# A Mamba-2 mixer between two LoRA layers: programs written out, and x transposed directly behind the mixing

## What is computed

```python
proj = hidden_states @ in_proj_w.T                     # 512 -> 18560
gate, xBC, dt = jnp.split(proj, [INTER, INTER + CONV_DIM], axis=-1)
conv = causal depthwise convolution of xBC, 4 taps, + conv_b
xBC = jax.nn.silu(conv)
x, Bm, Cm = jnp.split(xBC, [INTER, INTER + NG * SS], axis=-1)
dt = jnp.clip(jax.nn.softplus(dt + dt_bias), DT_MIN, DT_MAX)
cs = jnp.cumsum(dt * A)                                # by head
scores = (C . B) * exp(cs_l - cs_s), lower triangle    # by head
y = scores @ (x * dt) + x * D
yg = y * jax.nn.silu(gate)
out = (yg * rsqrt(mean(yg ** 2) in each of 8 groups)) * norm_w
x = x + out @ out_proj_w.T
```

## Time and profile before

| | us |
|---|---|
| runs before, median of 3 | 1664.43 |
| lowest and highest | 1662.55, 1666.53 |
| profiled execution | 1663.83 |
| its span | 1662.0 |
| its mean granted TensorE clock | 0.985 of full speed |

### The profile page before, as it was taken

One profiled execution on the slowest core, in us unless ns is written; L12 is line 12 of the kernel. 1 busy time (PEld: TensorE's weight loads), 2 busy tenths in 40 slices (PEclk: granted clock), 3 DMA queues, 4 the chain that ended last, 5 costly groups with the idle time before them and its releaser, 6 DMA issues. The chain is left out here.

```text
span 1662.0 us, 27199 instructions
## 1 busy us (share of the span) xinstructions
PE 1579.7 (95%) x8296; PEld 1228.1 (74%) x8296; DVE 1314.3 (79%) x1689; ACT 1025.0 (62%) x2122; POOL 1071.0 (64%) x790
## 2 busy tenths in 40 slices
PE   6979999999999999999999999999999999999879
PEld 4657777777777777777777777777777777777657
DVE  6689877887788777887788777887788777887565
ACT  4467766656666666666666665666666565666431
POOL 2028884777658784777648784787657784788520
PEclk9899999999999999999999999999999999999979
DMA  3033322223222222222222221222222221222011
GB/s 115 1 108 118 106 77 71 89 91 90 71 77 90 88 80 70 90 90 71 78 89 89 67 89 58 97 89 84 77 73 90 89 90 58 89 90 83 20 39 51
DMA packets 73709, 132.16 MB, mean 80 GB/s; under 512 B 10944, under 2 KB 10944, under 8 KB 73280
## 3 DMA queue, kind: packets, MB, share of 16 engines
q1 hardware_dynamic: 73536, 130.09, 23.8%
HBM read 127.44 MB, written 2.62 MB: 78 GB/s over the span
## 5 line engine op out<-in xcount | busy, mean ns | idle before, releaser
L159 PE MATMUL bank<-h_hi,mx_w_hi 128*128 128x512 f32 x1152 | 481.1, 418 | 23.7 <-issue 21.8
L161 PE MATMUL bank<-h_hi,mx_w_lo 128*128 128x512 f32 x1152 | 455.5, 395 | 0.0
L160 PE MATMUL bank<-h_lo,mx_w_hi 128*128 128x512 f32 x1152 | 452.2, 393 | 0.0
L839 POOL TENSOR_TENSOR mx_w_lo<-mx_w_raw,mx_w_hi 128x512 fp32r<-128x512 f32 x144 | 365.1, 2536 | 112.2 <-ACT mx_w_hi L834 112.1
L1113 ACT ACTIVATE mx_mix<-mx_csb,mx_gncs 128x256 f32<-128x256 f32 x512 | 219.1, 499 | 277.6 <-PE bank L1480 254.2
L892 DVE SCALAR_TENSOR_TENSOR mx_acc<-bank,mx_cw,mx_acc 128x510 f32<-128x510 f32 (+2 forms) x480 | 356.5, 743 | 30.5 <-ACT mx_acc L877 19.2
L1267 DVE TENSOR_TENSOR mx_mix<-mx_mix,mx_cbt 128x1536 f32<-128x1536 f32 x128 | 356.2, 2783 | 0.0
L159 PEld LDWEIGHTS bank<-h_hi,mx_w_hi 128*128 128x128 f32 x1152 | 217.8, 189 | 83.2 <-issue 46.3
L1285 DVE SCALAR_TENSOR_TENSOR mx_y<-mx_acc,mx_dh,bank 128x512 f32<-128x512 f32 x128 | 95.7, 747 | 207.6 <-PE bank L1480 185.1
L1038 POOL TENSOR_TENSOR mx_y<-mx_y,mx_sg 128x512 f32<-128x512 f32 x128 | 213.5, 1668 | 69.4 <-DVE mx_y L1285 60.1
L161 PEld LDWEIGHTS bank<-h_hi,mx_w_lo 128*128 128x128 f32 x1152 | 217.4, 189 | 50.0
(11 more groups left out here) (163 smaller groups left out, 2183.9 us busy)
## 6 DMA issues: line engine op xcount, KB each, us to landing
mx_csb<-cs_rows SPq DMA_DIRECT2D x128, 512.0 KB, 4.0
mx_w_raw<-in_w_in SPq DMA_DIRECT2D x144, 256.0 KB, 4.1
mx_wo_raw<-in_w_out SPq DMA_DIRECT2D x64, 256.0 KB, 4.2
res<-in_x SPq DMA_DIRECT2D x8, 256.0 KB, 3.6
f_base_raw<-in_base_wt SPq DMA_DIRECT2D x2, 1024.0 KB, 5.9
out<-res SPq DMA_DIRECT2D x8, 256.0 KB, 2.0
f_a_raw<-in_lora_a SPq DMA_DIRECT2D x2, 256.0 KB, 3.0
f_lb_raw<-in_lora_b SPq DMA_DIRECT2D x2, 256.0 KB, 6.7
```

Source lines behind the costliest of these rows:

```text
L159: nc.tensor.matmul(out, w_hi, x_hi, start=first, stop=False)
L160: nc.tensor.matmul(out, w_hi, x_lo, start=False, stop=False)
L161: return nc.tensor.matmul(out, w_lo, x_hi, start=False, stop=last)
L839: self.nc.gpsimd.tensor_tensor(self.w_lo[:, w % 3, :, :], self.w_raw[:, w % 3, :, :], self.w_hi[:, w % 3, :, :].bitcast(F32), ALU.subtract ...
```

## The change

It does five things.

1. `loop_halves` is replaced by `groups_in_turn`: the programs of TensorE, ScalarE and VectorE are written out for all 8 groups, with no loop.
2. TensorE: `transpose_x` comes first in a step, directly behind the mixing of the step before, and the projection of unit st + 5 behind it. Unit 5 is projected in the tail, between `project` 4 and the second `b_dot_c`, and no longer in step 0.
3. VectorE: the `silu_conv` of a step's start moves to the end of the step before, behind `silu_gate`: step st now makes the SiLU of unit st + 5 (in step 15: of unit 0 of the next group). That of unit 4 closes the tail.
4. VectorE: `inverse` moves from the end of the tail to step 0 of the next group, behind its `silu_conv`.
5. ScalarE's tail: `evacuate` 3 goes ahead of `tanh_conv` 2, and `evacuate` 4 ahead of `round_w` 3.

```diff
-        def loop_halves(eng, steps, tail):
-
-            half = XT + 1
-            steps(0, range(half), True)
-            with eng.Fori(0, NG - 1) as g:
-                steps(g, range(half, STEPS), True)
-                tail(g, True)
-                steps(g + 1, range(half), True)
-            steps(NG - 1, range(half, STEPS), False)
-            tail(NG - 1, False)
+        def groups_in_turn(steps, tail):
+
+            for g in range(NG):
+                steps(g, g + 1 < NG)
+                tail(g, g + 1 < NG)
...
@@ scalar, tail
                     evacuate(g + 1, 2)
+                    evacuate(g + 1, 3)
                     tanh_conv(g + 1, 2)
-                    evacuate(g + 1, 3)
                     tanh_conv(g + 1, 3)
+                    evacuate(g + 1, 4)
                     ip.round_w(act, g + 1, 3)
-                    evacuate(g + 1, 4)
                     tanh_conv(g + 1, 4)
...
@@ vector, before the steps, in a step, in the tail
+            silu_conv(0, 4)
...
                     if st >= 1:
                         skip_y(g, st - 1)
-                    silu_conv(g, st + 4)
                     make_mix(g, st)
                     scale_x(g, st)
...
                     silu_gate(g, st)
+                    if here or more:
+                        silu_conv(gn, un)
                     if st % 2 == 1:
                         split_wo(g, st // 2)
+                    if st == 0 and not first(g):
+                        inverse(g - 1)
...
                 if more:
-                    silu_conv(g + 1, 0)
                     head_constants(g + 1)
...
                     keep_bc(g + 1, 1)
-                    inverse(g)
+                    silu_conv(g + 1, 4)
...
@@ tensor, before the steps, in a step, in the tail
             ip.project(pe, 0, 4)
+            ip.project(pe, 0, 5)
             b_dot_c(0, 1)
...
-                    if st + 1 < STEPS:
+                    transpose_x(g, st)
+                    if 0 < st < STEPS - 1:
                         ip.project(pe, g, st + 5)
-                    elif more:
+                    elif st == STEPS - 1 and more:
                         ip.project(pe, g + 1, 0)
-                    transpose_x(g, st)
                     project_gate(g, st)
...
                     ip.project(pe, g + 1, 4)
+                    ip.project(pe, g + 1, 5)
                     b_dot_c(g + 1, 1)
```

More of the change, by code:

```diff
@@ L1170, in _, with steps @@
             tanh_conv(0, 4)
-            def steps(g, these, more):
-                for st in these:
+            def steps(g, more):
+                for st in range(STEPS):
                     here = st + 1 < STEPS
@@ L1232, in tail @@
                     next_ln.root(act, 1)
-            loop_halves(act, steps, tail)
+            groups_in_turn(steps, tail)
         @block.vector
@@ L1419, in tail @@
                     add_group(NG, 7)
-            loop_halves(dve, steps, tail)
+            groups_in_turn(steps, tail)
         @block.tensor
@@ L1493, in project_out @@
                     pe.wait_ge(s["gsum"], 1 + TT * g + p - 1)
-                elif isinstance(g, int) and g == NG:
+                elif g == NG:
                     pe.wait_ge(s["gcopy"], 1 + TT * g - 1 + p)
@@ L1550, in tail @@
                     project_out(NG, 7)
-            loop_halves(pe, steps, tail)
+            groups_in_turn(steps, tail)
 def program(nc, x, w_in, w_dt, conv_w, conv_b, dt_bias, d_skip, norm_w, w_out, base_wt, router_wt, lora_a, lora_b,
```

## The result

| | before | after |
|---|---|---|
| median of 4 runs, us | 1665.48 (1662.55 to 1670.57) | 1625.80 (1624.96 to 1627.01) |
| profiled execution, us | 1663.83 | 1627.01 |
| its span, us | 1662.0 | 1625.2 |

The ratio is 0.9759, with a 95% interval of 0.9734 to 0.9785. The change gains 36.8 us between the two spans and 39.7 us between the medians. 27.7 us were forecast, counted from the profiled execution, and the time lies 2.2 us under the range.

The account below looks back on a forecast made before the run. The prediction took TensorE, busy 1579.7 of 1662.0 us, to bound the kernel. From the profiled execution, 1663.83 - 24.6 - 5.3 - 1.45 + 3.65 = 1636.1 us, with a range of 1628 to 1643.

Parts of the forecast that it names:

- Part 1, jumps: Loop jumps between steps 8 and 9 of groups 1 to 6: writing loops out removes stalls and slow stretches, -24.6 us.
- Part 2, joints: Seven joints of two groups: project 5 fills a gap and transposes come earlier, 0.75 us each, -5.3 us.
- the chain of unit 5: Joint, step 1: ScalarE's table loads, root and evacuation delay unit 5's SiLU to 661.2, limiting the gain to 0.75 us.
- Part 3: Step 15 of group 7: the transposes' wait for the SiLU of unit 19 goes, -1.45 us.
- Part 4, chain in group 0: Steps 0 to 7 of group 0: without output projection the SiLU chain makes steps 8.15 us, +3.65 us.
- Part 4, switches: Transposes behind the mixing in 120 steps: five uncovered weight loads before and after, 0 us, bounds ±0.06 us a step.
- Cheaper in front: Rival: the chain doesn't bind in group 0 and joints gain 1.1 us, 1630 us; chance 0.12.
- The dear switch: Rival: going from mixing straight to transposes costs extra 120 times, 1648 us at 0.10, 1672 at 0.30; chance 0.07.

Follow-up runs that it names:

- e1: The kernel before with its three loops written out and no instruction moved; 1639.58 us, ratio 0.9853.
- e2: The changed kernel with the loops of the kernel before kept, all moves made; 1659.09 us (median of ten), ratio 0.9973.
- e6: The changed kernel with the reciprocal (`inverse`) back in VectorE's tail, ahead of the SiLU of unit 4; 1638.51 us, ratio 0.9851.
- e11: The changed kernel with the transposes between the gate projection and the output projection; 1609.61 us (one run).
- e3: The changed kernel with the transposes of x behind the projection again in every step, VectorE's SiLU left in its new place; 1626.51 us, ratio 0.9782.
- e4: The changed kernel with the transposes behind the projection in steps 0 to 7 of group 0 alone; 1620.33 us, ratio 0.9749.
- e8: The changed kernel with the SiLU of unit 4 ahead of the copy of B·C in VectorE's tail; 1626.13 us, ratio 0.9787.
- e9: The changed kernel with ScalarE's root behind the tanh of unit 5 and VectorE's reciprocal moved to step 1; 1625.24 us, ratio 0.9774.

## Why the prediction was wrong, point by point

**Part 1, jumps: right**, size included (e1). The clause that three slow stretches go with them is right as well. What it missed is that a jump's price depends on what surrounds it: 31.1 us in e2.

**Part 2, joints: right mechanism, 2.3 us too small in all.** TensorE's wait before the transposes came out as 1.71 us (1.7 to 1.8 by the working) and that in step 1 as 0.13. Of the 1.09 us of a joint, 0.16 came with the written-out programs (e1), which I had left out, and 0.93 with the moves, for which 0.75 was forecast. Of these 0.18 us, 0.08 are the order on TensorE, which makes step 1 as much shorter as the ordinary step, and about 0.1 the chain of unit 5, which I had put too late (mixing 0 to 1 is 0.16 us over 10.29, where 0.25 was forecast).

**Part 3: right.**

**Part 4, chain in group 0: right chain, 1.7 us too small.** Steps of 8.15 us were forecast and measured. The term that failed is mostly the first step: 5.86 us between transposes 0 and 1, measured 7.01. In front of it TensorE now has its idle time in one piece (2.57 us instead of 0.35 and, further up, 2.74), and the clock is at 1.2 GHz from 115.6 to 119.0, in which step 0's gate projection runs. e6, whose program in group 0 is the same, shows what that costs. Its clock stayed at 2.4 GHz behind the same wait (113.14 is the start of its first transposes):

```profile
113.80:117.20 3.40, 3.40 (x21) 2.46 (x22) 3.33 (x5) 2.98 (x8) 2.08 (x2) 1.00 0.00 0
...
119.41 0.66 PE L1446 MATMUL bank<-ident,mx_acc 128*128 128x128 f32 x4 [1.39 <-DVE mx_acc L1244]
```

Transposes 1 come 6.27 us behind transposes 0 there, and mixing 8 after 72.49 us instead of 73.27. So 0.8 us of the 1.7 is the clock. Another 0.4 is the chain of step 0 itself (6.27 against 5.86), and 0.3 is the step from transposes 7 to 8 (8.48 us against 8.15). I had written that the joint before group 0 gains nothing, and did not ask what else the gap's new place does.

**Part 4, switches: this step failed, and it is the cause of the miss.** I counted weight loads left uncovered, five before and five after, and took 0 with ±0.06 us a step as bounds. It was -0.080, 8.3 us in all, and that is nearly the whole distance from the forecast (parts 2 and 4 miss by 2.3 and 1.7 us in opposite directions). Start-to-start distances of single matmuls in one ordinary step of each trace, in ns, give this:

| order | step | mixing | transposes | products of 512 columns |
|---|---|---|---|---|
| before: mixing, P, T, G, O | 10367 | 1451 | 355 | 2861 + 2862 + 2838 |
| changed: mixing, T, P, G, O | 10286 | 1451 | 415 | 5583 + 2837 |
| e11: mixing, P, G, T, O | 10307 | 1451 | 355 | 5581 + 2920 |

P, G and O are projection, gate projection and output projection, T the transposes. Two input products in one unbroken run take 5583 ns instead of 5723. That is 140 saved. 87 of it are the first distance behind the transposes (314 instead of 227), 47 the rest of the second product, whose next distances are mostly 228 to 236 ns before they settle at 227, and 7 the first product. On the other side, transposes behind the mixing cost 60 ns more (169 instead of 109 for their first), and transposes in front of the output projection cost that 83. My count priced a product's and a transposition's uncovered load alike, and it left out the run-in of the next matmuls. e3 shows that the order is the cause (10.37 us with everything else equal), and e11 that breaking up P and G is what matters, not the mixing's neighbourhood. Why the distances need several matmuls to settle I could not show.

**Rivals.** None came about as a whole. "Cheaper in front" had the joint right (1.1 us) and group 0 wrong, where the chain binds; its 1630 us is nearer than the forecast, but it holds no price for the order in the ordinary step either. The dear switch had the wrong sign in sum: transposes behind the mixing do cost 60 ns more, but a projection there pays too (338 ns to its second matmul, 314 behind transposes), and the unbroken run saves more.

## What to carry to other kernels

Where TensorE is full, read the start-to-start distances of single matmuls around every change of kind: a block of transposes between two products over the same inputs cost 140 ns here beyond its own time. Its new place behind the mixing took 60 of them back, which leaves 8 us over the kernel. In front of the output projection the block cost 83 ns. That this product has other inputs may or may not be the reason; no run separates it. When a producer is moved off a consumer's path, ask of every phase which work still covers the chain. Here the same order won in 104 steps and lost in the eight that had no output projection, and one condition on the group gave most of both (e4, with 2.06 us of wait where the orders meet). And before one wait at a joint is shortened, look for the one just behind it: e8 and e9 were worth nothing or 1 us alone, and 8 together.

## What the runs showed of the hardware that I had not expected

- TensorE's clock stood at 2.4 GHz behind all seven waits of 1.71 us in the changed kernel's joints, and fell to 1.2 GHz behind five of seven waits of 2.28 to 2.34 us in e6. It also fell behind one of seven waits of 1.90 us in e2, and behind three of nine of 2.57 to 2.61 us at the start of group 0. A fall cost 1.56 us a joint.
- A jump of the loop cost TensorE 3.1 to 3.6 us of waiting in the kernel before and up to 4.21 us in e2, where other work stands around it.
- Of two elementwise operations on VectorE and GpSimd, the one that starts first kept its own speed and the other was stretched: 1.75 and 2.73 us, or 1.30 and 2.48.
